# Order of values, maxima and output transposes in the attention slots of a two-layer transformer kernel

## Time and profile before

| | |
|---|---|
| median of 3 runs | 1537.91 us (1537.15 to 1542.62) |
| the profiled execution's own time | 1533.47 us |
| its span, first to last instruction | 1531.7 us |
| TensorE (PE) busy | 1111.0 us, 73% |
| VectorE (DVE) busy | 735.2 us, 48% |
| ScalarE (ACT) busy | 481.5 us, 31% |
| GpSimd (POOL) busy | 165.7 us, 11% |
| mean granted TensorE clock | 0.871 |

### The profile page before, as it was taken

The page is one execution under the profiler, slowest core; times in us unless marked ns, Lnnn a source line. Parts: engine busy times, 40 slices in busy tenths (PEclk is TensorE's granted clock), DMA queues, the critical chain, the costliest instruction groups (busy, mean ns, idle before and its releaser), DMA issues. The chain is left out here.

```text
span 1531.7 us, 21860 instructions
## 1 busy us (share of the span) xinstructions
PE 1111.0 (73%) x7926; PEld 741.1 (48%) x7926; DVE 735.2 (48%) x1746; ACT 481.5 (31%) x971; POOL 165.7 (11%) x219
## 2 busy tenths in 40 slices
PE   1012597888898979998988996873509999999920
PEld 0011364544565446664556654742505776667720
DVE  7996244566444676448665564243301222222236
ACT  1000132345444434363535542420002323333210
POOL 3781100000000000000000000000070000000043
PEclk9999998788899989699978897975559999999975
DMA  8011102000003000020001200102941101111023
GB/s 252 0 29 29 38 13 69 15 1 14 1 29 100 4 15 1 15 90 28 1 1 42 90 1 14 56 0 87 377 181 35 35 28 35 35 35 35 25 79 96
DMA packets 65479, 77.99 MB, mean 51 GB/s; under 512 B 14960, under 2 KB 57600, under 8 KB 65248
## 3 DMA queue, kind: packets, MB, share of 16 engines
q1 hardware_dynamic: 61040, 63.08, 12.9%
q0 software_dynamic: 4336, 13.50, 2.7%
HBM read 55.86 MB, written 20.71 MB: 50 GB/s over the span
## 5 line engine op out<-in xcount | busy, mean ns | idle before, releaser
L1407 DVE TENSOR_REDUCE mx<-scores_ps 128x4 f32<-128x1024 f32 (+1 forms) x160 | 187.1, 1169 | 137.6 <-PE scores_ps L891 92.6
L1230 ACT ACTIVATE pt<-turned_ps 128x1024 f32<-128x1024 f32 (+1 forms) x160 | 157.9, 987 | 148.6 <-PE turned_ps L913 102.9
L1852 PE MATMUL x_ps<-x_w,x_xtT 128*128 x312 | 142.6, 600 | 0.8 <-ACT x_xtT L1892 0.5
L1863 PE MATMUL x_ps<-x_w,x_hT 128*128 x624 | 141.2, 379 | 2.1 <-ACT x_hT L1907 2.1
L1998 DVE COPY x_raw<-x_ps 128x512 f32<-128x512 f32 x78 | 54.0, 692 | 167.4 <-PE x_ps L1852 167.4
L1907 ACT ACTIVATE x_hT<-x_ps,x_b1c 128x128 f32<-128x128 f32 x312 | 84.9, 383 | 142.2 <-PE x_ps L1870 142.2
L1863 PEld LDWEIGHTS x_ps<-x_w,x_hT 128*128 128x128 f32 x624 | 115.6, 190 | 16.8 <-issue 2.7
L841 POOL COPY vpad<-v 128x64 f32<-128x64 f32 x64 | 16.3, 286 | 738.0 <-PE ps L952 595.0
L903 PE MATMUL turned_ps<-q,k 32*128 32x256 f32 x512 | 73.6, 363 | 24.6 <-DVE mx L1407 13.9
L351 PE MATMUL s_ps<-s_pw,s_cs 64*32 64x64 f32 x512 | 15.8, 310 | 102.1 <-DVEq L298 96.0
L903 PEld LDWEIGHTS turned_ps<-q,k 32*128 32x128 f32 x512 | 45.7, 210 | 84.2 <-issue 49.4
(11 more groups left out here) (352 smaller groups left out, 2044.4 us busy)
## 6 DMA issues: line engine op xcount, KB each, us to landing
wexp<-in_L_ffn_w SPq DMA_DIRECT2D x16, 1024.0 KB, 5.4
x_w<-in_L_ffn_W SPq DMA_DIRECT2D x16, 1024.0 KB
x_slots<-s_zero POOLq DMA_DIRECT2D x1, 4992.0 KB, 20.1
x_xt<-x_slots SPq DMA_DIRECT2D x39, 128.0 KB, 2.1
y_slots<-x_y SPq DMA_DIRECT2D x39, 128.0 KB, 1.7
ha<-h SPq DMA_DIRECT2D x16, 256.0 KB, 3.1
h<-s_out SPq DMA_DIRECT2D x32, 64.0 KB, 1.8
x<-hb SPq DMA_DIRECT2D x8, 256.0 KB, 2.5
```

The source lines that it names most:

```text
L1230: sc.activation(pt[v.index // 2 % (PT_RING // 2)][:, :, 0:wide], turned_ps[:, :, 0:wide], ACT.Exp)\
L1407: v.tensor_reduce(mx[:, u.group % 2, 0:blocks, u.n:u.n + 2].rearrange("p b n -> p n b"), scores_ps[:, :, 0:blocks * (P if u.causal else T) ...
L1852: last = mm(ps[h][:, :], xtT[:, i % 2, c, :], w1[:, bass.ds(expert, 1), c, h * HALF:(h + 1) * HALF], start=c == 0, stop=c == DC - 1)
L1863: last = mm(ps[4 + (i - 1) % 2][:, 0:D], hT[:, (i - 1) % 2, f, :], w2[:, bass.ds(last_expert, 1), f, :], start=f == 0, stop=f == FT - 1)
```

## The change

On TensorE `values` moves from the end of the slot to directly behind `x_slot`, in front of `maxima_t` and `outputs_t`. On ScalarE the copy of `ps[4]` to `acc` moves in front of the copy of the maxima row. No instruction is added or removed, and no lag, buffer or wait condition changes.

```diff
@@ TensorE, x_stream
             for s in range(len(plan.slots)):
                 x_slot(s)
+                u = plan.last(s, AV_LAG)
+                if u and u.ends_quad:
+                    values(u)
                 u = plan.last(s, MT_LAG)
                 if u and u.ends_group:
                     maxima_t(u.group)
                 u = plan.last(s, AV_LAG + 2)
                 if u and u.ends_quad:
                     outputs_t(u)
-                u = plan.last(s, AV_LAG)
-                if u and u.ends_quad:
-                    values(u)
                 yield
@@ ScalarE, x_stream
             for s in range(len(plan.slots)):
+                u = plan.last(s, AV_LAG + 1)
+                if u and u.ends_quad:
+                    act.wait_ge(sg("av_done"), u.index + 1)
+                    if u.step >= 2:
+                        act.wait_ge(sg("o_full"), u.step - 1)
+                    sc.copy(acc[u.step % 2][:, :], ps[4][:, 0:T]).then_inc(sg("acc"), 1)
                 u = plan.last(s, MT_LAG)
                 if u and u.ends_group:
                     act.wait_ge(sg("mt_full"), u.group + 1)
                     if u.group >= 2:
                         act.wait_ge(sg("st_full"), 8 * (u.group - 1))
                     sc.copy(mrow[:, u.group % 2, :], ps[5][:, T:]).then_inc(sg("mrow"), 1)
-                (the copy to acc stood here)
                 vs = plan.two(s, ST_LAG)
```

More of the change, by code:

```diff
@@ L1215, in x_stream @@
                     sc.copy(mrow[:, u.group % 2, :], ps[5][:, T:]).then_inc(sg("mrow"), 1)
[L1216 to L1221, removed]
                 vs = plan.two(s, ST_LAG)
```

## The result

The changed kernel takes 1553.71 us, median of 5 runs (1552.34 to 1555.37), against 1537.91 us before. The ratio is 1.0091, 95% interval 1.0067 to 1.0116 (all ratios in this text are near those of the means; that of these two medians is 1.0103). The forecast of 1533.6 us was wrong in sign, and 1553.7 us lies outside the range of 1525 to 1542. The profiled execution took 1552.34 us with a span of 1550.6 us, against 1533.47 and 1531.7 us before: 18.9 us more of each. The loss lies in `main_loop`: at its last projection, 1047 us into the span of the kernel before (not 1000, as I wrote ahead of the prediction), the kernel after is 20.7 us behind, counted from each one's first score matmul. `expert_mixture` behind it takes 402.5 us before and 401.5 us after, from TensorE's first to its last matmul there.

What follows compares the result with a forecast made beforehand. TensorE's instruction list was taken to set the pace. Terms 4.8 + 1.8 - 0.9 gave 5.7 us, three quarters kept as 4.3: 1537.9 - 4.3 = 1533.6 us, 8-in-10 range 1525 to 1542.

Steps and rivals of the forecast that it cites:

- the seams: TensorE's block changes in main_loop: 8.2 us saved in 41 slots without mask, 3.4 us lost in 17 masked ones.
- ScalarE's order: In slots with maxima, the earlier acc copy lets exponentials start 0.26 us sooner; seven TensorE waits shorten, 1.8 us.
- A: Rival, chance 0.20: the full-array load behind the output transposes waits after all, so that saving is nothing; 1537 us.
- C: Rival, chance 0.13: VectorE waits at the reciprocal for later transposes, delaying what follows; 10 us less 4.3, 1543 to 1544 us.
- the prediction's own sign (beyond 13.9): Sign for C: TensorE's waits for VectorE's maxima grow beyond 13.9 us, with VectorE's waits for output transposes far longer.
- B: Rival, chance 0.22: more is kept, with half-clock slots and ScalarE's evictions gaining too; about 10 us, 1528 us.
- It widens the range and is no case.: On the granted clock, 0.82 to 0.96 by stretch: half-clock windows may move a few us either way; no chance given.
- one sum for two stages: TensorE's list in main_loop: 8.2 us gained without mask less 3.4 lost with mask, 4.8 us shorter.

Runs made afterwards that it cites:

- act_first: Only ScalarE's copy order changed against the kernel before, TensorE keeping the old order: 1541.55 us, ratio 0.9978.
- new_order_x0: New TensorE order only in slots with causal scores, old order elsewhere, ScalarE as in the changed kernel: 1554.18 us, 1.0105 of the kernel before.
- after_again: The changed kernel itself run once more, for a second profile: 1556.79 us, 1.0069 of the kernel before.
- new_order_x1: New TensorE order only in slots without causal scores, old order elsewhere, ScalarE as in the changed kernel: 1539.30 us, 0.9972 of the kernel before.
- after_tail: The changed kernel plus dummy matmuls in waits of the last pair's tail: 1545.80 us, 1.0057 of the kernel before.
- x1_tail: new_order_x1 plus dummy matmuls in waits of the last pair's tail: 1530.35 us, 0.9957 of the kernel before.
- after_tail_again: after_tail repeated on another chip: 1537.18 us, 1.0025 of the kernel before.
- x1_tail_again: x1_tail repeated on another chip: 1520.84 us, 0.9945 of the kernel before.
- before_tail: The kernel before plus dummy matmuls in waits of the last pair's tail: 1533.69 us, 0.9966 of the kernel before.
- run 23: Not a numbered run but a count: the unchanged kernel before, run 23 times on one chip, median 1533.6 us.

## Why the prediction was wrong

**Right: the seams.** At 2.4 GHz the X1 slots gained 5.5 us in 33 slots (forecast 6.2 in 31), and the stretches of X0 lost 4.8 (forecast 3.4 + 0.9). Of the slots that should gain, 5 ran at 1.2 GHz in both kernels and took 0.2 us more in all, where the sum had assumed 0.20 us less for each; they are too few to say what a seam is worth there.

**Right: ScalarE's order** (1.44 us in the wait that was forecast at 1.45; 2.9 us less in all waits for the exponentials, forecast 1.8; act_first 2.5 us ahead at 745 us).

**Refuted: A.** The load behind the transposes has no idle time, so the rule of the Trainium skill that was set against it ("TensorE: Matmul & The Clock Gate", "Part 3: Packing small matmuls — row/col tiling") does not hold for this seam: the load starts at 462.99 us, the transposes' matmuls last from 462.83 to 463.27 us, their end being the profile's model. **Refuted: C**, although its sign is the one that came: VectorE waited 51 times in place of 16, for 35.5 us more, and TensorE's waits for maxima grew only from 13.9 to 17.4 us. By the prediction's own sign (beyond 13.9) that is C, but its price is 3.5 us and not 10, and new_order_x0 is slow with 14.5. **B** did not come either.

**Wrong: "It widens the range and is no case."** This is the step that failed. The granted clock stood in every row, between 0.82 and 0.96, and I took its windows for something that the edit does not move. The comparison puts 17.0 of 19.7 us on places whose clock changed, and the runs bear it out in three ways. The new order in X0, some 4 us of seams, costs 12.7 to 16.8 us in the means on three chips (after_again against new_order_x1, after_tail against x1_tail, after_tail_again against x1_tail_again). Dummy matmuls, which shorten nothing on TensorE's list, take the loss away where they hold the clock: 8 to 12 us in the tails of the profiles that had lost them, and the 6 us at 565 us. And act_first, 2.5 us ahead at 745 us, loses 10 in the tail with TensorE's old order, at a granted clock of 0.73 there against 0.81 before.

**Also wrong: one sum for two stages.** Gain in X1 and loss in X0 had been worked out apart and then added, as if a microsecond were worth the same everywhere. By the runs, the loss in X0 is worth about four times its size (1.0105, 1.0048 to 1.0163 of 4 runs, so 7 to 25 us for 4), while X1's gain with ScalarE's comes to 0.9972 (0.9941 to 1.0002), which is not told apart from nothing.

**The reference point.** The profile of before, against which all was measured, is a favourable one: its tail takes 114 us at a granted clock of 0.81, where the other kernels without filler take 122 to 128. Part of the 18.9 us is this. after_tail, which does not lose in the tail, is still 9.5 us behind at the loop's end, and 1.0057 (1.003 to 1.0085).

**Open.** None of the longer runs of the kernel before was profiled. That they have a slower tail is only likely (before_tail has none of them), and x1_tail keeps its longer runs in spite of the filler. Which small shifts cost and which don't was not found. Profiles in which the granted clock changes at the same distance from the loop's start repeat one another to 0.1 to 0.3 us; others of the same kernel differ by several (x1_tail and x1_tail_again 3.2 us at 745 us, after and after_again 3.8). The Trainium skill ("TensorE: Matmul & The Clock Gate", "Part 1: The HAM clock gate (the "warmup" mystery)") says that the throttle's watching runs free of the kernel's start, so that one kernel differs from run to run; these profiles agree, by the 3.2 and 3.8 us.

## What to carry to other kernels

Where TensorE's granted clock moves between its levels during the work, a change of a few us can have its effect multiplied or turned round: before adding up seams, see in the rows which stretches run at 1.2 GHz and what wait stands before them, and give the clock a case of its own in the forecast. Move an order only where the seams gain, stage by stage: here values first in X1, the old order in X0, and dummy matmuls in the tail gave 0.9945 (0.9913 to 0.9978) where the order everywhere gave 1.0091. The filler's own part in this was not told from nothing (0.9972 without it). And profile a kernel more than once before taking one profile as the point from which to count: the profile before missed a tail that is 10 us longer in act_first, with the same order on TensorE.

## What the hardware showed beyond that

- The same 8 matmuls (128x64) took 1.00 and 1.81 us, with 0.5 us more of idle time ahead of the slower ones (1.90 in place of 1.40 us); the lower level then lasted 14 us.
- Twelve dummy matmuls of 512 columns (2.75 us) at the start of a wait of 8 us left the block behind it at 1.2 GHz (1.97 us for 8, as without them). In the tail, the same kind of matmul in several waits in a row brought the X1 projection of the last pair from 6.14 back to 3.32 us in the changed kernel, and left it at 5.0 us in the kernel before.
- A full-array weight load started 0.17 us after the load of full-array transposes, while their matmuls still ran (462.99 us, matmuls to 463.27 by the profile's model). Between 32-column values and a full-array load 0.41 us stood idle, between full-array transposes and 64-column values 0.17, between a bfloat16 mask and such values 0.21.
- Two 128x256 copies on ScalarE of 0.37 and 0.38 us started 0.27 us apart; moving one out of the chain shortened a wait by 0.27 us, not by 0.38.
- One kernel on one core, run 23 times on one chip, took 1531.0 to 1536.9 us 17 times and 1542.0 to 1547.4 us 6 times, with nothing in between. On three other chips the same kernel had no such gap, and medians from 1532.0 to 1546.1 us.
